# A gated cross-attention and mixture-of-experts block: half of the shared feed-forward moved into the attention pass, scores as 32-row products

## What is computed

```
q = layernorm(x) @ Wq.T + bq ; k, v = ctx @ Wk.T + bk, ctx @ Wv.T + bv      (16 heads of 32)
att = q k^T / sqrt(32), masked by padding and by position ; prob = softmax(att)
x = x + tanh(g_xattn) * (prob v)
z = layernorm(x)
shared = (silu(z @ shared_gate) * (z @ shared_up)) @ shared_down             (512 -> 512 -> 512)
p = softmax(z @ router) ; the two largest of 8 are kept, as coef
routed = sum over e of coef[e] * ((silu(z @ gate[e]) * (z @ up[e])) @ down[e])   (512 -> 256 -> 512)
out = x + tanh(g_ffn) * (routed + shared)
```

## Time and profile before

| what | us |
|---|---|
| median of three runs | 1142.1 |
| profiled execution, its own time | 1144.73 |
| its span, first to last instruction | 1143.0 |
| TensorE busy in the span | 1046.4 |
| VectorE busy | 788.8 |
| ScalarE busy | 498.1 |
| POOL busy | 444.1 |
| mean granted TensorE clock | 0.952 of 2.4 GHz |

### The profile page before, as it was taken

The page is one execution under the profiler, slowest core; times in us unless marked ns, Lnnn a source line. Parts: engine busy times, 40 slices in busy tenths (PEclk is TensorE's granted clock), DMA queues, the critical chain, the costliest instruction groups (busy, mean ns, idle before and its releaser), DMA issues.

```text
span 1143.0 us, 30439 instructions
## 1 busy us (share of the span) xinstructions
PE 1046.4 (92%) x9392; PEld 761.0 (67%) x9393; DVE 788.8 (69%) x2813; ACT 498.1 (44%) x1010; POOL 444.1 (39%) x654
## 2 busy tenths in 40 slices
PE   5898989999999999870799999999999999999997
PEld 4587768777877877760355555555555888888885
DVE  5899778888888888774576666666665445455455
ACT  2465546666666666641354444444443111111111
POOL 4344546666666666543221122112110322232322
PEclk9998889999999999965899999999999999999999
DMA  7463563334433323430433333433342555545554
GB/s 267 184 237 137 161 175 96 94 94 94 94 94 94 94 94 94 112 89 24 134 116 113 116 110 119 120 110 117 114 127 68 165 160 162 174 158 170 151 173 138
DMA packets 76735, 147.02 MB, mean 129 GB/s; under 512 B 20912, under 2 KB 23088, under 8 KB 73872
## 3 DMA queue, kind: packets, MB, share of 16 engines
q1 hardware_dynamic: 46512, 66.01, 19.5%
q0 software_dynamic: 12896, 35.58, 11.5%
q10 hardware_dynamic: 17280, 44.83, 10.6%
HBM read 94.04 MB, written 52.35 MB: 128 GB/s over the span
## 4 chain that ended last, share of the span: by engine, by line
PE 61%; issue 11%; DVE 11%; POOL 8%; ACT 3%; DMA 3%; POOLq 1%; another core or an unknown queue 1%; SPq 0%; DVEq 0%; ACTq 0%
PE bank L1046 8%; PE bank L1048 8%; PE bank L1047 8%; PE bank L1038 7%; PE bank L1240 5%; PE bank L1241 5%; PE bank L1242 5%; PE bank L1091 4%; DVE arena L779 3%; PE bank L1111 3%; POOL arena L468 3%; PE bank L1251 2%; PE bank L1252 2%; PE bank L1253 2%; POOL token_of_row L504 2%
## 5 line engine op out<-in xcount | busy, mean ns | idle before, releaser
L1038 PE MATMUL bank<-ident,arena 128*128 128x128 f32 (+1 forms) x1336 | 169.4, 275 | 49.9 <-DMA arena<-normed_rows,arena 25.6
L1038 PEld LDWEIGHTS bank<-ident,arena 128*128 128x128 f32 (+1 forms) x1336 | 144.7, 139 | 88.7 <-issue 67.4
L1241 PE MATMUL bank<-arena,weights 128*128 128x128 f16 x1024 | 174.9, 218 | 0.1
L1240 PE MATMUL bank<-arena,weights 128*128 128x128 f16 x1024 | 174.9, 220 | 0.0
L1242 PE MATMUL bank<-arena,weights 128*128 128x128 f16 x1024 | 174.8, 218 | 0.0
L515 POOL DMA_INDIRECT arena<-normed_rows,arena x71 | 67.1, 946 | 251.8 <-PE bank L1038 234.6
L1046 PE MATMUL bank<-weights,arena 128*128 x426 | 162.0, 380 | 2.1 <-ACT arena L648 1.9
L1047 PE MATMUL bank<-weights,arena 128*128 x426 | 161.8, 380 | 0.0
L1048 PE MATMUL bank<-weights,arena 128*128 x426 | 161.8, 380 | 0.0
L1111 PEld LDWEIGHTS bank<-arena 128*128 128x128 f32 x1024 | 131.9, 199 | 38.0 <-issue 31.9
L1091 PE MATMUL bank<-arena 128*128 128x512 f32 x256 | 145.7, 675 | 7.7 <-DVE arena L779 7.0
(11 more groups left out here) (180 smaller groups left out, 2207.1 us busy)
## 6 DMA issues: line engine op xcount, KB each, us to landing
expert_rows<-arena ACTq DMA_DIRECT2D x71, 256.0 KB, 2.1
arena<-in_x SPq DMA_DIRECT2D x64, 256.0 KB
weights<-in_w_gu ACTq DMA_DIRECT2D x8, 1024.0 KB, 4.9
x_rows<-arena SPq DMA_DIRECT2D x32, 256.0 KB
normed_rows<-arena SPq DMA_DIRECT2D x32, 256.0 KB
normed_transposed<-arena SPq DMA_DIRECT2D x32, 256.0 KB
arena<-normed_transposed SPq DMA_DIRECT2D x32, 256.0 KB
arena<-x_rows SPq DMA_DIRECT2D x32, 256.0 KB
```

What stands on the lines that cost most here:

```text
L1038: last = t.transpose(dst[:, c * P:(c + 1) * P], src[:, c * P:(c + 1) * P], (ident16 if src.dtype == F16 else ident)[:, :])
L1240: t.matmul(dst, shared(c, part, 0, dc), x_hi_c, start=(c == 0), stop=False)
L1241: t.matmul(dst, shared(c, part, 0, dc), x_lo_c, start=False, stop=False)
```

## The change

- **Odd tiles' shared feed-forward in pass 1.** The shared gate/up and down weights are loaded, scaled and split at the start of pass 1, and stay in SBUF. For each odd tile pass 1 also forms up (half an iteration's worth in each of two iterations), gate, silu and the down product. Silu is written with Tanh: (tanh(g/2) + 1) * up * g. The result, with the gate's factor, is added to the tile's row block of x1 in DRAM: SP loads x1 again into `s_x1`, VectorE adds, SP stores `s_base` over it. The lag of pass 1 grows from 8 to 11, the written-out head from 12 to 16 iterations. The transposed tile is stored for even tiles only.
- **Scores.** `kbd` goes. The columns of Wq and Wk are put in another order on the host, so that a group of four heads sits at the same 32 rows; a head's scores are one f32 product of 32 rows and 128 columns, 16 a tile. Groups k and k+1 alternate, so that neighbouring products use other rows and another bank. `scores(0)` and `scores(2)` do two groups each, and wait for the maxima of the group before.
- **Banks.** Transposed probabilities now use one bank, mixed values one, and gate/down and up of the shared part one each.
- **Orders.** The bodies of TensorE, VectorE and ScalarE are ordered anew.
- **Plan.** The last eight tiles have row-list buffers of their own. The counts, the drains and the plan come at iteration 39, ahead of the last three iterations. The expert down weights are loaded at iteration 35 by SP into the space of the attention buffers; two of their four chunks are split before pass 2 and two in its first two iterations.
- **Pass 2.** The shared down weights' load, peak exchange and split are gone from it.
- **Pass 3.** 16 iterations. Each does the shared part of one even tile and the sums of an even and an odd tile: two x1 loads, four gathers with one index copy, five VectorE operations instead of four per tile, two stores. The factor of the gate is in the probabilities and in `f_back`.

```diff
+        P_BANK, A_BANK, G_BANK, U_BANK = 4, 5, 6, 7
+        LQ, LS = 2, 3
+        LV, LX1, LX2, LR, LK = LS + 1, LS + 2, LS + 3, LS + 4, LS + 5
+        LU, LG, LD, LB = LX2 + 1, LX2 + 2, LX2 + 3, LX2 + 4
+        LAG1, LAG2, LAG3, SPAN2 = LB + 1, 4, 4, 4
+        HEAD1 = 16
...
 SP, pass 1
+                n, j, u = tile(J, v, LB)
+                if live(n, NT - 1) and u == 1:
+                    store_base(j)
+                n, j, u = tile(J, v, LD - 1)
+                if live(n, NT) and u == 1:
+                    hold(sp, sp_passed, (x1_out[u], 16 * (j + 1)))
+                    hold(sp, sp_passed, (s_base_done, j))
+                    sp.dma_start(s_x1, x1_dram[bass.ds(j * P + S, P), :]).then_inc(s_x1_here, 16)
...
+                if it == ATTENDED_IT:
+                    sp.wait_ge(av_done, EC * NT)
+                    for i in range(DOWN_CHUNKS):
+                        sp.dma_start(down_raw(i), down_src(i)).then_inc(down_in[i // 2], 16)
...
 POOL, pass 3
+                    hold(pool, pool_passed, (f_idx_ready, n + 1), (f_out_ready, B * (n - 1)))
+                    for b in range(B):
+                        for k in range(TOP):
+                            at = b * TOP + k
+                            g.indirect_dma_start(f_y[u][b][k], None, y_dram,
+                                                 bass.IndirectOffsetOnAxis(ap=f_idx[u][:, at:at + 1], axis=0)).then_inc(f_y_here[u], 16)
...
 ScalarE, pass 1
+                    a.activation(s_h_hi, s_t, ACT.Copy, scale=1.0 / LO_UP).then_inc(f_h_hi_done, 1)
...
+                    a.activation(s_t, bank[G_BANK][:, :], ACT.Tanh, scale=half_back[:, :]).then_inc(f_act_ready, 1)
...
 VectorE, pass 1
+                    d.scalar_tensor_tensor(s_h_lo, s_h_hi, -LO_UP, s_t, ALU.mult, ALU.add).then_inc(f_h_lo_done, 1)
...
+                    d.scalar_tensor_tensor(s_t, s_t, 1.0, bank[U_BANK][:, :], ALU.add, ALU.mult).then_inc(s_t_done, 1)
...
+                    d.scalar_tensor_tensor(s_t, bank[G_BANK][:, :], 2.0 ** -43, s_t, ALU.mult, ALU.mult).then_inc(f_h_ready, 1)
...
+                    d.scalar_tensor_tensor(s_base, bank[G_BANK][:, :], f_back[:, :], s_x1, ALU.mult, ALU.add).then_inc(s_base_done, 1)
...
+                if it == 5:
+                    dve.wait_ge(down_peak_in, 16 * DOWN_CHUNKS)
+                    for i in range(DOWN_CHUNKS):
+                        largest(4 + i, slot(3 + i))
+                if it == SHARED_IT + 1:
+                    shared_low(0)
+                    shared_low(1)
...
 TensorE, pass 1
-                        t.matmul(bank[2 + k % 2][:, :], q_t[u][:, k * P:(k + 1) * P], kbd[:, u, k, :],
-                                 start=True, stop=True).then_inc(s_done, 1)
+                        for c in range(EC):
+                            for g in (k, k + 1):
+                                rows = slice(g * D, (g + 1) * D)
+                                mm = t.matmul(bank[2 + g % 2][:, c * T:(c + 1) * T], q_t[u][rows, c * P:(c + 1) * P],
+                                              k_t[rows, c, u, :], start=True, stop=True)
+                                if c == EC - 1:
+                                    mm.then_inc(s_done, 1)
...
                 turn_probs(0)
+                scores(0)
+                shared_up(0)
+                shared_up(1)
+                mix_values(0)
                 turn_probs(1)
...
+                shared_rest(0)
+                mix_values(1)
+                turn_probs(2)
                 scores(2)
+                shared_rest(1)
...
 TensorE, pass 3
-                if live(n, NT):
+                if live(n, HALF):
                     pe.wait_ge(f_x_here[u], 16 * (j + 1))
-                    need(pe, f_h_ready, n - 1)
+                    pe.wait_ge(f_h_ready, FIRST + n - 1)
...
             pipeline(pe, body2, SLOTS, LAG2, SPAN2, beside=beside2)
-            pipeline(pe, body3, NT, LAG3, start=LAG2)
+            pipeline(pe, body3, HALF, LAG3, start=LAG2)
```

809 lines of the change are left out of this document (458 added, 351 removed).

## The result

The changed kernel took 1133.25 us (median, 1120.29 to 1136.29) beside 1142.55 us for the kernel before on the same chip: a ratio of 0.9894 [0.9854, 0.9934], 1.06% faster. The forecast was 1068 us, and 1133.25 lies outside its range of 1032 to 1112. The profiled execution took 1132.7 us (span 1130.9), so the two profiled spans differ by 12 us where the forecast had 74.

What follows compares the result with a forecast made beforehand. The prediction took TensorE as the bound, fully in the last pass, with clock and wait losses in the first. Its terms, -130.1 + 3 + 38 + 14 + 2 - 1 = -74, took 1142.1 to 1068 us, range 1032 to 1112.

Steps and rivals of the forecast that it cites:

- Last pass, -130.1 + 3: Last pass: 16 iterations of 8.13 us go, -130.1 us; later first gathers and extra work at the end add 3.
- Rival (d): Last pass bound by DMA at 10 us a pair: +30 us, 1098 us in all; chance 0.05.
- 19 loop iterations, +38: First pass loop: 16.3 us an iteration, +1.98 over 19 iterations, so +38 us.
- the 0.4 I kept: First pass loop: of 1.7 us an iteration lost to clock and waits, 0.4 us was expected to remain.
- Head, +14: Iterations 4 to 15: 176 us against 165.0, +11, and +3 for a peak exchange at iteration 4.
- busy share of 0.88: Head: VectorE's 154.6 us of work divided by 0.88 gave 176 us, iteration 5's late passes partly covered in it.
- over 0.96 in the first pass: Sign that the prediction is right: TensorE's granted clock in the first pass above 0.96.
- Drain and plan, +2: Between first and second pass: 8 us of shared work not hidden, VectorE's 5.67 us wait gone; net +2 us.
- Second pass, -1: Second pass: the shared down weights' peak exchange (2.41 us TensorE wait) goes, two splits come: -1 us.
- (a): First pass scores: paired products fully overlap, 1.72 us, 25 us less, 1043 us in all; chance 0.22.
- (b): First pass scores: no overlap and array emptying, 4.24 us; 1111 us, or 1136 with today's losses kept; chance 0.19.
- (c): First pass scores: f32 loads not pulled ahead, 0.30 us a record, +210 us, 1278 us in all; chance 0.06.

## Why the prediction was wrong, point by point

- **Last pass, -130.1 + 3.** The pace was right. The first and last of its products by line, 980 to 1131 us of the changed kernel (shortest, median and longest ns, then the first and the last start; the last count is of one shape):

```profile
L1219 PE MATMUL bank<-arena,weights x512: 219/219/311, 986.0 to 1117.9; 128*128 128x128 f16 x171
...
L1231 PE MATMUL bank<-weights,arena x64: 379/379/379, 1000.0 to 1123.5; 128*128 128x512 f16 x64
```

Four products of L1231 belong to a pair, so 15 pairs and a rest lie between the first and the last: less than (1123.5 - 1000.0) / 15 = 8.2 us a pair, against 8.13 a tile; DMA at 0.89 and 297 GB/s stayed hidden, where I had 93% and 291 GB/s. The entry and the end were mis-sized: 3 us forecast, 121.2 gained of 130.1, so 9, of which 4.6 are the wait that the later x1 loads removed. Rival (d) did not come here. In two sets of runs a slow last pass did come (163.4 to 173.8 us; in the repeat of the changed kernel 10.0 a pair), at its price, but with stops of TensorE and DMA less busy, not more.
- **19 loop iterations, +38.** Right: 294.6 / 18 = 16.37 us an iteration, forecast 16.3. In part that is luck, since its parts were off both ways: scores 2.32 us, not 2.65, and 0.4 us more lost in waits than the 0.4 I kept. TensorE is the bound there and its clock is 0.99.
- **Head, +14.** This is the step that failed: +55.7. I worked out VectorE's added work, divided by a busy share of 0.88 and let "three iterations between stages cover" the heap. That takes VectorE as the one limit. Without peaks 27 us go, with even peaks and filled waits, and all of VectorE's work kept, 27 go too. So for this half of the loss the size of VectorE's work was not the price; the price is that TensorE stands behind it, falls to the lower clock and then needs nearly twice the time for what it has to do. The sum had no term for the clock in the head: the mean clock to iteration 16 was 0.83, and 0.93 in the kernel before. The paragraph on VectorE said of the loop that TensorE's "clock has fewer pauses to fall in": that is true from iteration 16, and the sign that I named for it, over 0.96 in the first pass, failed because of the head (0.92 up to iteration 34). The other 28 us of the head stay when the peaks go. Unread products in iterations 4 to 8 took 3.2 us off two of these; the short scores alone cost the kernel before 1.8%, but in the loop and not in its head, so what share of the 28 they have is not shown.
- **Drain and plan, +2.** Failed as well: +16. I gave the 4 MB load "about 12 us beside the row stores" and counted nothing for what it does to the 256 KB stores queued behind it (17.21 us), for which VectorE waits 9.9 us. Moving that load alone gave 4.7 us back, the other order of the plan 5, since the landing of the last scatter then grew to 16.3 us, from 8.7 in the kernel before. The other 9 or so of these 14 us stay open.
- **Second pass, -1.** +1; the products there are the same.
- **Rivals.** (a) and (b) bounded the scores well, and the truth lay between: 2.32 of 1.72 to 4.24. (c) had the wrong mechanism; the one that cost most, a lower clock in the head, was none of my rivals, though my own first paragraph had counted 0.57 us an iteration lost to it.

**What stays open.** Besides half of the head and the rest of the drain: stops of all engines at once, of 1 to 5 us, the longer ones with the lower clock behind them, stand in iterations 9, 15 and 17 of the changed kernel's first trace and in 8, 13 and others elsewhere. In the changed kernel at 264 us, and in the one without peaks at 245 us:

```profile
264.02 0.27 PE L1165 MATMUL bank<-ident,arena 128*128 128x128 f32 x1 [1.60 <-issue]
...
264.05 0.17 DVE L920 TENSOR_SCALAR arena<-arena 128x4 f32<-128x4 f32 x1 [2.29 <-remote]
...
264.35 0.60 ACT L646 ACTIVATE arena<-bank 128x512 f16<-128x512 f32 x1 [4.88 <-remote]
```

```profile
245.15 0.22 PE L1273 MATMUL bank<-arena 128*128 128x128 f16 x1 [4.21 <-issue]
...
245.16 0.17 DVE L928 TENSOR_SCALAR arena<-arena 128x4 f32<-128x4 f32 x1 [5.06 <-issue]
```

"Issue" and "remote" mean that the profile shows no releaser. The stops don't come from the peaks (they remain without them) nor from SP's new steps. Another suspect is the program itself: its first iterations are written out, longer than before, and fetching them might stop the engines. No run tried that, but the traces say something. The page's third section names two DMA queues of the kind "instruction". They move 38 packets in the first 308 us of the changed kernel and none from 309 to 542, in the loop; and all its stops of the first pass that hold TensorE, VectorE and ScalarE at once for over 0.5 us lie before 308. That fits. But two other runs have such a stop in the loop, the repeat of the kernel before at 297 us and the first run with unread products at 331 us, where no packet of these queues stands between 290 and 310 or between 310 and 350 us:

```profile
299.20 0.17 PE L1161 MATMUL bank<-seen,ones 128*128 128x8 f16 x1 [1.88 <-issue]
```

```profile
333.82 0.22 PE L1226 MATMUL bank<-arena,weights 128*128 128x128 f16 x1 [2.42 <-issue]
```

So fetching, if these packets are the fetches, can't be the reason for all of them. Nor is the slow last pass explained: it came only with the changed kernel's last pass, which keeps the DMA engines at 0.89 where the former one had 0.51, but the run with half the gathers did not meet it. Between 1062 and 1150 us of the slow one 23 of TensorE's stops stand and no packet of the instruction queues.

## What to carry to other kernels

A saving on TensorE in a stretch where another engine is nearly level with it can make the kernel slower: here a short wait in every iteration came with a lower clock that cost more than the saving. Bring the work that fills the gap into the same iterations, or measure the saving by itself first. Price preparation that rides in a main loop by who stands behind it in one iteration, and spread it before adding anything; products without a reader cost time ahead of work that is ready, and paid here only together with the even peaks. Before putting megabytes of load on a queue, look for the small store on it that someone waits for.
